# A decoder layer's cross-attention: context loaded with channels first, split into two parts on GpSimd instead of transposed on TensorE

## What is computed

```
B, N, C = x.shape            # 16, 56, 256
H = 16; D = C // H           # 16 heads of 16 channels
q = _w8a8_linear(x, wq, bq).reshape(B, N, H, D).transpose(0, 2, 1, 3)
k = (cond @ wk.T + bk).reshape(B, L, H, D).transpose(0, 2, 1, 3)    # cond: (16, 1500, 256)
v = (cond @ wv.T + bv).reshape(B, L, H, D).transpose(0, 2, 1, 3)
scores = jnp.einsum('bhnd,bhld->bhnl', q, k) * inv_sqrt_d + mask[:, None]
attn = jax.nn.softmax(scores, axis=-1)
o = jnp.einsum('bhnl,bhld->bhnd', attn, v)
return _w8a8_linear(o.transpose(0, 2, 1, 3).reshape(B, N, C), wo, bo)
```

## Time and profile before

| what | us |
|---|---|
| median of 3 runs (940.9 to 945.22) | 944.49 |
| the profiled execution | 937.71 |
| its span, first to last instruction | 936.0 |
| PE busy (share of the span) | 805.2 (86%) |
| DVE busy | 569.6 (61%) |
| ACT busy | 555.3 (59%) |
| POOL busy | 71.3 (8%) |

### The profile page before, as it was taken

The page is one execution under the profiler, slowest core; times in us unless marked ns, Lnnn a source line. Parts: engine busy times, 40 slices in busy tenths (PEclk is TensorE's granted clock), DMA queues, the critical chain, the costliest instruction groups (busy, mean ns, idle before and its releaser), DMA issues. The chain is left out here.

```text
span 936.0 us, 19297 instructions
## 1 busy us (share of the span) xinstructions
PE 805.2 (86%) x7771; PEld 675.9 (72%) x7771; DVE 569.6 (61%) x1090; ACT 555.3 (59%) x945; POOL 71.3 (8%) x84
## 2 busy tenths in 40 slices
PE   4945689989999999999999999999999989848855
PEld 3533478777877887778787878788888878726644
DVE  3795466656665566565746665666556656636746
ACT  2513156767676667676767676677767775624423
POOL 1021000000000000000000000000000000061633
PEclk8965799999999999999999999999999999977978
DMA  6009566675757575757676667676767674560231
GB/s 180 14 20 279 142 141 170 151 186 131 185 131 179 131 179 137 172 144 164 151 158 151 159 158 167 161 160 165 164 160 162 164 165 95 122 173 8 83 96 40
DMA packets 70279, 133.34 MB, mean 142 GB/s; under 512 B 24112, under 2 KB 53464, under 8 KB 70104
## 3 DMA queue, kind: packets, MB, share of 16 engines
q1 hardware_dynamic: 66016, 123.39, 55.5%
q0 software_dynamic: 2048, 7.34, 2.9%
q10 hardware_dynamic: 2128, 1.38, 0.5%
HBM read 52.59 MB, written 5.57 MB: 62 GB/s over the span
## 5 line engine op out<-in xcount | busy, mean ns | idle before, releaser
L1296 ACT ACTIVATE probsT<-ps_T 125x448 f32<-125x448 f32 x376 | 191.6, 545 | 171.4 <-PE ps_T L1168 156.6
L1398 DVE CUSTOM_DVE_ANT_0 scores<-ps_scores,mask_sb 112x1500 f32<-112x1500 f32 x128 | 219.7, 1717 | 71.7 <-PE ps_scores L1146 64.2
L1168 PE MATMUL ps_T<-ident,scores 112*128 112x112 f32 (+1 forms) x1536 | 196.2, 264 | 25.0 <-ACT probsT L1296 23.0
L1168 PEld LDWEIGHTS ps_T<-ident,scores 112*128 112x128 f32 (+1 forms) x1536 | 173.8, 147 | 52.6 <-ACT probsT L1296 31.6
L1284 ACT ACTIVATE scores<-scores,shift 112x1500 f32<-112x1500 f32 x128 | 197.3, 1542 | 2.7 <-issue 2.1
L1134 PE MATMUL ps_proj<-wkvT,room 128*125 128x256 f32 x1152 | 158.8, 287 | 7.1 <-DVE v_sb L1376 7.0
L1126 PE MATMUL ps_proj<-room,wkvT 128*128 128x500 f32 x576 | 159.2, 413 | 4.0 <-DVE room L1381 3.3
L1134 PEld LDWEIGHTS ps_proj<-wkvT,room 128*125 128x125 f32 x1152 | 145.4, 187 | 16.0 <-DVE v_sb L1376 7.2
L1385 DVE SCALAR_TENSOR_TENSOR room<-ps_proj,xbk,room 128x500 fp32r<-128x500 f32 x96 | 70.8, 738 | 105.0 <-ACT room L1279 104.8
L1146 PE MATMUL ps_scores<-k_stack,q_stack 96*112 96x500 f32 x384 | 118.0, 415 | 6.7 <-DVE shift L1398 6.1
L1126 PEld LDWEIGHTS ps_proj<-room,wkvT 128*128 128x128 f32 x576 | 104.7, 195 | 26.2 <-issue 5.2
(11 more groups left out here) (257 smaller groups left out, 569.8 us busy)
## 6 DMA issues: line engine op xcount, KB each, us to landing
k_stack<-room SPq DMA_DIRECT2D x384, 187.5 KB, 4.0
ctx_rows<-in_ctx SPq DMA_DIRECT2D x48, 500.0 KB
mask_sb<-in_mask_BxSxS_ff SPq DMA_DIRECT2D x32, 328.1 KB
q_stack<-q_hi SPq DMA_DIRECT2D x32, 112.0 KB, 5.6
q_hi<-k_stack SPq DMA_DIRECT2D x4, 448.0 KB, 3.8
q_lo<-k_stack SPq DMA_DIRECT2D x4, 448.0 KB, 4.0
q_stack<-q_lo SPq DMA_DIRECT2D x16, 112.0 KB, 5.5
x_sb<-in_x SPq DMA_DIRECT2D x1, 896.0 KB, 6.4
```

The costliest lines, as they stand in the source:

```text
L1168: last = nc.tensor.transpose(ps_T[0:wide, (TB * t + k) % 2, j * PN:(j + 1) * PN], scores[:, t % 2, key:key + wide], keep["ident"][0:PN, 0:PN])
L1296: nc.scalar.activation(probsT[:, t % 2, k * TC:(k + 1) * TC], ps_T[0:LT, (TB * t + k) % 2, 0:TC * PN].rearrange("p (j n) -> p j n", j=TC), ...
L1398: nc.vector.tensor_tensor_reduce(out=split(scores[:, t % 2], NC), in0=ps_scores[0:PN, :, 0:LC], in1=split(mask_sb[:, a], NC), scale=-1.0, ...
```

## The change

The input array is handed over with channels first, (16, 256, 1500), and `load_chunk` loads 500 columns for both channel halves on 128 partitions. The X units are gone from PE, ACT and DVE. The high and low parts of a chunk (`cT_hi`, `cT_lo`) are made from the loaded fp32 chunk in SBUF: for batch 0 by ACT and DVE, for batches 1 to 15 by GpSimd (`split_context`, a copy to fp32r and a subtraction, 128x1000 each). GpSimd takes a chunk when it has landed and when the last K or V unit of the batch before that reads the chunk is done on PE (`readers_done`). K and V units wait for `ctx_lo` instead of for X units. The table of units has twelve entries, one in each slot. SP's load of a chunk for batch b+2 waits until GpSimd has split that chunk of batch b+1. The wait for the bias row ahead of L1068 becomes a wait for two rows.

```diff
+def context_of(keep):
+    return split(keep["context"][:, 0:KT * L], KT)
 def load_chunk(sp, io, keep, b, c):
-    sp.dma_start(split(keep["context"][0:LT], NL)[:, c * TC:(c + 1) * TC],
-                 io["ctx"][b, c * LC:(c + 1) * LC].rearrange("(j p) d -> p j d", p=LT)).then_inc(keep["ctx_in"][c], 16)
+    sp.dma_start(context_of(keep)[:, :, c * LC:(c + 1) * LC],
+                 io["ctxT"][b, :, c * LC:(c + 1) * LC].rearrange("(m p) l -> p m l", p=P)).then_inc(keep["ctx_in"][c], 16)
 UNITS = [
-    ([("X", 0, 0), ("X", 0, 1)], [("X", 1, 0), ("X", 1, 1)], [("X", 2, 0), ("V", 0, 0), ("X", 2, 1)]),
-    ([("K", 0, 0)], [("K", 0, 1)], [("K", 0, 2), ("V", 1, 0)]),
-    ([("V", 2, 0)], [("V", 3, 0)], [("V", 4, 0)]),
-    ([("K", 1, 0)], [("K", 1, 1)], [("K", 1, 2), ("V", 5, 0)]),
+    ([("V", 0, 0)], [("V", 1, 0)], [("V", 2, 0)]),
+    ([("K", 0, 0)], [("K", 0, 1)], [("K", 0, 2)]),
+    ([("V", 3, 0)], [("V", 4, 0)], [("V", 5, 0)]),
+    ([("K", 1, 0)], [("K", 1, 1)], [("K", 1, 2)]),
 ]
-FIRST = [("X", 0, 0), ("X", 0, 1), ("K", 0, 0), ("X", 1, 0), ("X", 1, 1), ("K", 0, 1), ("X", 2, 0), ("X", 2, 1), ("K", 0, 2),
-         ("V", 0, 0), ("V", 1, 0), ("V", 2, 0), ("V", 3, 0), ("K", 1, 0), ("K", 1, 1), ("K", 1, 2), ("V", 4, 0), ("V", 5, 0)]
+FIRST = [("K", 0, 0), ("K", 0, 1), ("K", 0, 2), ("V", 0, 0), ("V", 1, 0), ("V", 2, 0), ("V", 3, 0),
+         ("K", 1, 0), ("K", 1, 1), ("K", 1, 2), ("V", 4, 0), ("V", 5, 0)]
-SCORES_AFTER = {12: 0, 14: 1}
+SCORES_AFTER = {6: 0, 8: 1}
-PREPARE_AT = {4: 1, 5: 2, 6: 3, 8: 4, 9: 5, 11: 6}
+PREPARE_AT = {0: 1, 1: 2, 2: 3, 3: 4, 4: 5, 5: 6}
+def chunk_of(u):
+    kind, p, q = u
+    return q if kind == "K" else (2 * p + 1) // TC
+def last_reader(at, c):
+    return max(n for u, n in at.items() if u[0] in "KV" and chunk_of(u) == c)
+        def readers_done(b, c):
+            if b == 1:
+                return last_reader(AT_FIRST, c) + 1
+            half, a = (b - 2) // 2, b % 2
+            return units_before(half, a) + last_reader(AT if a or half == 0 else AT_R, c) + 1
 # SP, in batch()
-                                sp.wait_ge(unit_in_psum, first + at[("X", c, 1)] + 1)
+                                sp.wait_ge(ctx_lo, NC * (b + 1) + c + 1)
                                 load_chunk(sp, io, keep, b + 2, c)
 # GpSimd
+                def split_context(b):
+                    for c in range(NC):
+                        e = slice(c * LC, (c + 1) * LC)
+                        pool.wait_ge(ctx_in[c], 16 * (b + 1))
+                        pool.wait_ge(unit_in_psum, readers_done(b, c))
+                        nc.gpsimd.tensor_copy(cT_hi[:, :, e], context[:, :, e]).then_inc(ctx_hi, 1)
+                        pool.wait_ge(ctx_hi, NC * b + c + 1)
+                        nc.gpsimd.tensor_tensor(cT_lo[:, :, e], context[:, :, e], cT_hi[:, :, e].bitcast(F32), ALU.subtract).then_inc(ctx_lo, 1)
-                pool.wait_ge(load["bo"], 16)
+                pool.wait_ge(load["bias"], 32)
+                for a in range(2):
+                    split_context(1 + a)
                 for i in range(NT - 2):
+                    for a in range(2):
+                        split_context(2 * i + 3 + a)
                     result_on_gpsimd(nc, pool, keep, i)
+                split_context(B - 1)
 # PE, in unit(); the branch of "X" is gone
+                    pe.wait_ge(ctx_lo, NC * n + chunk_of(u) + 1)
 # ACT and DVE, ahead of the units of FIRST
+                for c in range(NC):
+                    split_hi(0, c)
+                for c in range(NC):
+                    e = slice(c * LC, (c + 1) * LC)
+                    dve.wait_ge(ctx_hi, c + 1)
+                    nc.vector.tensor_tensor(cT_lo[:, :, e], context[:, :, e], cT_hi[:, :, e].bitcast(F32), ALU.subtract).then_inc(ctx_lo, 1)
 # the input
+        a = np.ascontiguousarray(inputs[name].transpose(0, 2, 1) if name == "ctx_2048" else inputs[name])
```

More of the change, by code:

```diff
@@ L606, in projection_room @@
     k_hi, k_lo = (room[:, 2 * n + k * L:2 * n + (k + 1) * L] for k in range(2))
-    context = split(keep["context"][0:LT], NL)
-    return cT_hi, cT_lo, k_hi, k_lo, context
+    return cT_hi, cT_lo, k_hi, k_lo, context_of(keep)
+def chunk_of(u):
[3 more added lines that the diff above has]
+    return max(n for u, n in at.items() if u[0] in "KV" and chunk_of(u) == c)
 def expert_room(keep):
@@ L937, in cross_attention_phase @@
         hi_ready = sem("hi_ready")
+        ctx_hi = sem("ctx_hi")
+        ctx_lo = sem("ctx_lo")
         unit_out = sem("unit_out")
@@ L947, in cross_attention_phase @@
         out_copied = sem("out_copied")
-        load = {n: sem(f"in_{n}") for n in ("wo", "w", "gate", "atom_w", "atoms", "imp", "bo", "bv")}
+        load = {n: sem(f"in_{n}") for n in ("wo", "w", "gate", "atom_w", "atoms", "imp", "bias")}
         ones_set = sem("ones_set")
@@ L999, in load_weights @@
                     sp.dma_start(atoms, io["L0_ffn_atoms"]).then_inc(load["atoms"], 16)
[L1000 to L1001 removed]
+                    sp.dma_start(bo_row, row(io["L0_xattn_bo"])).then_inc(load["bias"], 16)
+                    sp.dma_start(keep["bv_row"][:], row(io["L0_xattn_bv"])).then_inc(load["bias"], 16)
                 def k_out(first, at, m):
@@ L1019, in batch @@
                         if not load:
-                            sp.wait_ge(unit_in_psum, first + at[("X", NC - 1, 1)] + 1)
+                            sp.wait_ge(ctx_lo, NC * B)
                             load_indices(sp, io, keep)
@@ L1040, in _ @@
                 for c in range(NC):
-                    sp.wait_ge(unit_in_psum, AT_FIRST[("X", c, 1)] + 1)
+                    sp.wait_ge(ctx_lo, c + 1)
                     load_chunk(sp, io, keep, 1, c)
@@ L1113, in unit @@
                         return
[L1114 to L1121, removed]
+                    pe.wait_ge(ctx_lo, NC * n + chunk_of(u) + 1)
+                    if kind == "K":
                         c, e = slice(q * LC, (q + 1) * LC), slice(p * P, (p + 1) * P)
@@ L1260, in _, with split_hi @@
             def _(act):
+                def split_hi(b, c):
+                    e = slice(c * LC, (c + 1) * LC)
+                    act.wait_ge(ctx_in[c], 16 * (b + 1))
+                    if b > 0:
+                        act.wait_ge(unit_in_psum, readers_done(b, c))
+                    nc.scalar.activation(cT_hi[:, :, e], context[:, :, e], ACT.Copy).then_inc(ctx_hi, 1)
                 def unit_hi(first, at, n, u):
@@ L1268, in unit_hi @@
                     src = ps_proj[:, at[u] % 2, 0:LC]
[L1269 to L1280, removed]
+                    if q == 0:
+                        for k in range(GP):
+                            done = n * 16 * STACK if p == 0 else (n + 1) * 16 * STACK
+                            other = (1 - p) * GP + k
+                            if p == 1 or n > 0:
+                                act.wait_ge(k_in[other], done)
+                    nc.scalar.activation(k_hi[:, q * LC:(q + 1) * LC], src, ACT.Identity,
+                                         bias=keep["xbk"][:, p:p + 1]).then_inc(hi_ready, 1)
                 def exponentials(b, t):
@@ L1378, in unit_rest @@
                     dve.wait_ge(hi_ready, n * NHI + (HI_FIRST if at is AT_FIRST else HI_AT)[u] + 1)
-                    if kind == "X":
-                        c = slice(p * LC, (p + 1) * LC)
-                        nc.vector.tensor_tensor(cT_lo[:, q, c], ps_proj[:, bank, 0:LC], cT_hi[:, q, c].bitcast(F32),
-                                                ALU.subtract).then_inc(unit_out, 1)
-                    else:
-                        c = slice(q * LC, (q + 1) * LC)
-                        nc.vector.scalar_tensor_tensor(out=k_lo[:, c], in0=ps_proj[:, bank, 0:LC], scalar=keep["xbk"][:, p:p + 1],
-                                                       in1=k_hi[:, c].bitcast(F32), op0=ALU.add, op1=ALU.subtract).then_inc(unit_out, 1)
+                    c = slice(q * LC, (q + 1) * LC)
+                    nc.vector.scalar_tensor_tensor(out=k_lo[:, c], in0=ps_proj[:, bank, 0:LC], scalar=keep["xbk"][:, p:p + 1],
+                                                   in1=k_hi[:, c].bitcast(F32), op0=ALU.add, op1=ALU.subtract).then_inc(unit_out, 1)
                 def masked_scores(b, half, a, t, before):
@@ L1504, in _ @@
                 dve.wait_ge(x1_bo_ready, 1)
-                dve.wait_ge(load["bv"], 16)
+                dve.wait_ge(load["bias"], 32)
                 def plain(half, a):
```

7 lines of the change are left out of this document (3 added, 4 removed).

## The result

The changed kernel takes 870.55 us (median of 4 runs, 866.43 to 871.36), the kernel before 942.69 beside it on the same chip (4 runs): ratio 0.922 [0.919, 0.926]. The forecast was 874, the range 852 to 912.

A forecast was written before the change was run, and what follows sets the result against it. It took the ring through k_hi and k_lo, just behind PE, to bound the changed kernel: span 936.0 - 63.5 - 10 + 5 = 867.5, 869 with 1.7 around it, plus 5 for runs: 874 us, range 852 to 912.

The forecast's parts named there:

- the ring: Loop: K halves written, copied by 12 DMAs, overwritten; 20.6 us a half, not 22.72, saving 63.5; chance 0.62.
- 13.1: Stack DMAs in the loop, first issue to ACT's release: 13.1 us in a free queue, rather than 14.9.
- ACT will wait in every half: Loop: ACT waits about 2 us for stack DMAs in every half, before once in two batches.
- even with R0 in the gap, 14.2 is under 14.7: Loop, between K units: PE's work with R0, 14.2 us, stays under the ring's 14.7, so R units hide.
- PE alone: Loop without X units: PE's own work takes 18.6 to 20.3 us a half, about 19.4 on average.
- PE is the bound: Rival, loop: DMAs take 12 us in a free queue, PE sets the pace, about 838 us; chance 0.09.
- Loads: Context loads on 128 partitions: should spread over all engines and be gone in 4 to 7 us, before the stack.
- a miss: Rival, loop: stack DMAs stay slow, 14.0 to 14.9 us, a half 21.6 to 22.4, total 900 to 925; chance 0.20.
- GpSimd: Split in the loop: 4.4 us a chunk, hidden; rival that it locks DVE's masked scores, 1000 us, slower 0.05.
- Ahead of the loop: Before the loop: first stack issue at about 98 instead of 108.55, 10 us less, between 4 and 13.
- its landing 4 to 5 us later: Ahead of the loop: the gate's store, put at 92, lands 4 to 5 us later, before 9.8.
- The clock: Loop, behind ACT's waits: slow parts of 8.99 instead of 7.51 us add 5 us, 0 to 15.

The follow-up runs named there:

- e2: Changed kernel with 16 instead of 12 stack DMAs in each half, the low part sent a fourth time: 1040.19 us, 1.121 of the kernel before.
- e3: Changed kernel with stack DMAs in two parts, the first third of the columns sent early, ACT waiting by part: 833.76 us, 0.900 of the kernel before.
- e1: Changed kernel with each context chunk loaded as two DMAs, partitions 0 to 124 and 125 to 127: 962.99 us, 1.036 of the kernel before.
- the repeat: The changed kernel unaltered, measured again on another chip: 871.28 us, 0.921 of the kernel before.
- e7: Changed kernel with the K and V units placed in the table as before, still without X units: 854.64 us, 0.921 of the kernel before.

## Why the prediction was right, point by point

- **The bound** was the ring, as said: 20.71 us a half against 20.6. In 20 of the 22 turns in which ACT waited, the DMAs took 12.7 to 13.3 us (13.1 said) and the part behind them 7.50 to 7.53 (7.51 said). e2 and e3 change the ring and leave PE's work alone, and the time moves with it. The price of a slow ring was taken too low at its top: the kernel before also has DMAs of 15.4 us (193.41 to 208.85), not only 14.88.
- **"ACT will wait in every half"** fell. It waited 22 times in 30, since the step "even with R0 in the gap, 14.2 is under 14.7" was too close to call. From the end of the last K unit on PE (203.0, not shown) to that of the first of the next half, where ACT starts (217.75), PE took 14.75 us, so every fourth half, with R0 in its gap, was PE's. It cost nothing: 20.67.
- **PE alone** at 19.4 a half: e3 shows 39.53 / 2 = 19.8. The gain left by the ring was smaller than I priced it, 0.9 us a half instead of 1.2. (The sum of the rival "PE is the bound" gives 830, or 837 with the 1.7 and the 5 of the main sum, where the text has 838.)
- **Loads**: quick, as said, and "13.1" rested on it rightly. I would have priced a miss at +54 us (900 to 925); e1 shows over 100.
- **GpSimd**: the copy took 1.02 us, not 2.2; the subtraction 2.33 (2.2 said); nobody waited. It locked no masked scores: 1716 ns in the mean beside 150.7 us of split, 1717 before. The lock is real elsewhere. DVE's L1513 (87.97) runs under GpSimd's L1101 (86.39 to 90.94) in the kernel after; the same instruction takes 0.24 us in the kernel before, where GpSimd is idle:

```profile
87.97 3.05 DVE L1513 TENSOR_SCALAR atom_pn<-atom_p,atom_rsum 8x64 f32<-8x64 f32 x1
```

- **Ahead of the loop**: -5.4, not -10. The step that failed is "its landing 4 to 5 us later". The store left at 92.13 as said (92) and landed after 9.6 us, as long as before. I had blamed a load on a third of the engines. What the windows of the changed kernel show there is full engines:

```profile
94.00:96.00 2.00, 2.00 (x6) 0.35 (x4) 0.00 (x0) 0.00 (x0) 0.00 (x0) 1.00 1.00 202
96.00:98.00 2.00, 2.00 (x15) 1.64 (x14) 0.00 (x0) 0.00 (x0) 0.00 (x0) 1.00 0.92 324
```

  A small store behind queued loads would wait for all of them; that this is the cause was argued, not tried. Behind it, 115.03 to 120.97 took 5.94 us instead of 4.71, after a stall of PE. In the repeat it took 4.71, but the first stack issue came at 104.15 instead of 102.08: in all 4.7 us less than before, so about 5 is what this stretch gave.
- **The clock**: I gave it 5 us. Two turns of 22 had a slow part behind the wait (9.09 and 9.04 us, 3 us in all). ACT had waited 2.80 and 3.62 us ahead of these two, and 1.4 to 2.8 ahead of the others. In the loops of e1 and e2 each of the turns with a wait of 4.4 to 6.9 was slow, and none of e1's four with 3.3 to 4.2.
- **The tail** behind the last stack got 5.9 us shorter, which no step had. There PE stands in short gaps in which the profile shows no releaser. The tail is 124.8 us in the repeat (874.7 - 749.91) and 109.3 in e7 (855.9 - 746.61), each on another chip, though neither changes that code. So 5.9 us less is within what it varies by, and isn't shown to be an effect of the change.
- **The sum**: loop and clock -58.5 said, -60.0 measured; ahead -10 said, -5.4; tail 0 said, -5.9. The total (864.7 against 867.5 us of span) is close because the last two errors cancel, which is luck; the loop, five sixths of the gain, was right by itself.

## What to carry to other kernels

When work is taken off the busiest engine, look for the loop that closes through a single buffer: its length, read once from a wait that it caused, gave the new time of a half to 0.1 us, while PE's removed work (84 us with its idle time) would have given the wrong one. If that loop decides, send the buffer's first part early and wait for it by part. And count a load's partitions: what it does to the transfers queued behind it can be worth more than its own time.

## What was unexpected of the hardware

- Loads of 125 partitions ahead of the 12 stack DMAs made these take 17.8 to 21.5 us instead of 12.9 (e1); beside them the loads' own packets fall from about 63 a us to 24 to 30.
- After a wait of ACT of 4.4 to 6.9 us, in which PE stands for most of the time, the granted clock was 0.55 to 0.63 in the 4 us windows looked at, and the next 7.5 us took 8.9 to 10.3 (e1, e2).
- GpSimd's copy with conversion took 1018 ns for 1000 columns, its subtraction 2331; a price by the number of operands would have been nearer than one by the nearest row.
